# A Fourier operator's 3x3 convolution: 64-column matmuls on a doubled halo, and 32x32 taps on a halo that holds each pixel once

## What is computed

```python
h = concatenate([grid, x], -1) @ P_w + P_b                  # 5 -> 32 channels
h = transpose(h, (0, 3, 1, 2))
for i in range(4):
    h_ft = rfft2(h)                                         # only 16x16 modes are used
    out_modes = einsum('bixy,ioxy->boxy', h_ft[:, :, :16, :16], w_c[i])
    spec = irfft2(out_modes, s=(64, 64))
    conv = conv_general_dilated(h, conv_w[i], (1, 1), 'SAME') + conv_b[i]    # 3x3, 32 -> 32
    h = leaky(spec + conv)
h = leaky(transpose(h, (0, 2, 3, 1)) @ Q1_w + Q1_b)
out = (h @ Q2_w + Q2_b)[..., 0]
```

## Time and profile before

| | us |
|---|---|
| median of 3 runs | 1379.96 (1377.09 to 1383.61) |
| the profiled execution | 1379.42 |
| its span | 1377.6 |
| TensorE busy | 1248.0 (91%) |
| VectorE (DVE) busy | 541.0 (39%) |
| ScalarE (ACT) busy | 493.1 (36%) |
| GpSimd (POOL) busy | 66.8 (5%) |

### The profile page before, as it was taken

How to read it: one execution, slowest core, us unless ns; L and a number is a source line. 1 busy time by engine, 2 the same in 40 slices (tenths; PEclk the granted TensorE clock), 3 DMA queues, 4 the chain that set the end, 5 groups by cost and what they waited for, 6 DMA issues and landing times. The chain is left out here.

```text
span 1377.6 us, 42277 instructions
## 1 busy us (share of the span) xinstructions
PE 1248.0 (91%) x19664; PEld 709.5 (52%) x19664; DVE 541.0 (39%) x553; ACT 493.1 (36%) x934; POOL 66.8 (5%) x122
## 2 busy tenths in 40 slices
PE   4899997999999998999999989999999943799955
PEld 2566664555555555545555554434444413489945
DVE  3656753333353334333353322110111104667785
ACT  1255654033333332233333333334444432425511
POOL 2000000000000000000000000011111110000000
PEclk9999998999999999999999999999999976979967
DMA  8354547667666776766666663556655407000000
GB/s 279 140 158 132 147 159 190 217 192 190 191 190 191 191 190 219 191 190 191 190 192 193 191 187 74 121 130 129 129 121 116 89 3 157 0 1 1 1 0 16
DMA packets 39359, 192.53 MB, mean 140 GB/s; under 512 B 16432, under 2 KB 16560, under 8 KB 17456
## 3 DMA queue, kind: packets, MB, share of 16 engines
q1 hardware_dynamic: 30224, 137.39, 40.3%
q0 software_dynamic: 8960, 52.44, 10.5%
HBM read 136.84 MB, written 52.95 MB: 138 GB/s over the span
## 5 line engine op out<-in xcount | busy, mean ns | idle before, releaser
L376 PE MATMUL psum<-halo,conv 128*64 128x512 f32 x2304 | 516.2, 598 | 2.8 <-DMA halo<-activations 2.6
L504 ACT ACTIVATE x_now<-psum,conv_bias 128x512 f32<-128x512 f32 x256 | 172.9, 688 | 525.4 <-PE psum L387 508.1
L376 PEld LDWEIGHTS psum<-halo,conv 128*64 128x64 f32 x2304 | 157.5, 136 | 322.0 <-issue 318.6
L574 DVE STREAM_TRANSPOSE ft<-psum 128x1024 f32<-128x1024 f32 x50 | 98.3, 1966 | 380.3 <-PE psum L290 380.3
L387 PE MATMUL psum<-dft,vt 128*32 128x128 f32 x8192 | 241.0, 273 | 0.7 <-issue 0.6
L387 PEld LDWEIGHTS psum<-dft,vt 128*32 128x32 f32 x8192 | 220.7, 110 | 39.0 <-issue 39.0
L597 DVE STREAM_TRANSPOSE vt<-psum 128x1024 f32<-128x1024 f32 x64 | 126.0, 1969 | 249.3 <-PE psum L352 249.3
L487 ACT ACTIVATE spec<-psum 32x128 f32<-32x128 f32 x384 | 147.2, 383 | 40.3 <-PE psum L303 36.4
L567 DVE STREAM_TRANSPOSE xt<-x_now 128x1024 f32<-128x1024 f32 x100 | 124.0, 1242 | 34.0 <-ACT x_now L504 28.2
L352 PE MATMUL psum<-zt,dft 64*32 64x256 f32 x2048 | 78.2, 380 | 5.4 <-DVE zt L590 5.4
L511 ACT ACTIVATE xt<-psum,q1b 128x512 f32<-128x512 f32 x64 | 40.5, 683 | 106.8 <-PE psum L401 106.8
(11 more groups left out here) (133 smaller groups left out, 776.5 us busy)
## 6 DMA issues: line engine op xcount, KB each, us to landing
activations<-x_now POOLq DMA_DIRECT2D x48, 1056.0 KB, 8.7
halo<-activations SPq DMA_DIRECT2D x192, 264.0 KB, 7.4
halo<-activations SPq DMA_DIRECT2D x192, 263.9 KB, 7.6
wspec<-in_spec SPq DMA_DIRECT2D x16, 1024.0 KB, 9.6
xcol<-in_xcol SPq DMA_DIRECT2D x16, 384.0 KB, 4.5
x_now<-in_ser SPq DMA_DIRECT2D x2, 1056.0 KB, 6.7
t_lq<-in_onehot SPq DMA_DIRECT2D x1, 2048.0 KB, 14.8
t_kr<-in_causal SPq DMA_DIRECT2D x1, 2048.0 KB, 24.9
```

Of the source, the lines that this page charges most:

```text
L376: mm(acc[u][64 * r:64 * r + 64, :], conv[:, l - 1, dy, :], rows[:, at:at + 16, 0:G], start=(dy == 0), stop=False, skip_group_check=True)
L504: copy(x_now[:, k, 16 * u:16 * u + 16, 0:G], acc[u].rearrange("p (i j) -> p i j", j=G), ACT.Prelu, bias=conv_bias[:, l:l + 1], alpha=SLOPE ...
L574: vec.transpose(ft[:].rearrange("p k c -> p c k"), rowed.rearrange("p a b -> p (a b)").rearrange("p (i c) -> p c i", c=C)).then_inc(s_ft, 1)
```

## The change

Three things change together. First, the convolution's form: each of the 9 taps is a matmul of 32 input channels by 32 output channels for each of the four pixel parities and each of the four banks, 144 matmuls a tile at the 16 positions of the array. Input parity f goes to output parity f ^ d, where d tells whether the tap changes the row parity (2) and the column parity (1); the taps of one d form a segment, with 4, 2, 2 and 1 taps for d = 3, 1, 2 and 0. So that the four parities of a bank fall on different array rows and columns, bank u keeps its parities in the order parity ^ u ("turn"), and spectral, rows_forward, the head and the loads follow that. The halo holds each pixel once, with the same partitions as x_now.

Second, the order on TensorE: the four segments stand between the other groups of the tile. Since a segment d > 0 writes the places that the one before wrote from other array rows, it waits for it (s_seg). taps(T, 3) writes all four banks and waits for all four evictions of tile T - 1. The banks 0 and 1 are reported as finished (s_acc) by taps(T, 0) together.

Third, the transfers: a tile is stored with 4 DMAs of 264 KB, one per bank, the last two not before the next tile's segment 3 is done. It is loaded with 16 DMAs of 66 KB, 8 after segment 1 of the tile before and 8 after its segment 2. The next layer's weights go out 1 MB at a time in the tiles p = 2, 4, 6 and 8, and negate, which needs them, stands at p = 12 and not at p = 8. head_read is one activation of 128 partitions, and it stands before all of the tile's evictions.

The diff, cut to its core:

```diff
-PAD = 2 * PITCH
-HALO = 2 * PLANE + PAD
+UNIT = 16 * PITCH
+TOP = 1 + 2 * PITCH
+HALO = TOP + PLANE + 2 * PITCH + 1
...
-            def load_halo(T):
+            def load_halo(T, units):
                 l, p = place(T)
-                k, src = T % 2, T - PAIRS
-                sp.wait_ge(s_store[src % 2], 16 * (src // 2 + 1))
...
-                                     ).then_inc(s_halo[k], 16)
+                k = T % 2
+                for u in units:
+                    for f in range(4):
+                        g = 32 * (f ^ turn(l - 1, u))
+                        sp.dma_start(halo[32 * f:32 * f + 32, k, TOP + UNIT * u:TOP + UNIT * u + UNIT],
+                                     x_d[p, g:g + 32, UNIT * u:UNIT * u + UNIT]).then_inc(s_halo[k], 16)
...
-            sp.wait_ge(s_zero, 3)
-
...
-                    load_halo((l + 1) * PAIRS)
+            sp.wait_ge(s_zero, 2)
+
+            sp.wait_ge(s_mix, 4)
+            for p in range(2, PAIRS):
+                sp.wait_ge(s_acc, 4 * (p - 2) + 4)
+                load_columns(p)
+                if p % 2 == 0 and p // 2 <= 4:
+                    load_weights(1, p // 2 - 1)
+            for T in range(PAIRS, NL * PAIRS):
+                l, p = place(T)
+                src = T - PAIRS
+                sp.wait_ge(s_store[src % 2], 64 * (src // 2 + 1))
+                if T < PAIRS + 2:
+                    load_halo(T, range(4))
+                else:
+                    sp.wait_ge(s_seg, 3 * (T - 1 - PAIRS) + 2)
+                    load_halo(T, (0, 1))
+                    sp.wait_ge(s_seg, 3 * (T - 1 - PAIRS) + 3)
+                    load_halo(T, (2, 3))
+                if l < NL - 1 and p in (2, 4, 6, 8):
+                    if p == 2:
+                        sp.wait_ge(s_mix, 4 * l + 4)
+                    load_weights(l + 1, p // 2 - 1)
...
             def store(X):
-                pool.wait_ge(s_x, 4 * X + 4)
-                pool.dma_start(x_d[X % PAIRS], x_now[:, X % 2].rearrange("p i j -> p (i j)")
-                               ).then_inc(s_store[X % 2], 16)
+                for u in range(4):
+                    pool.wait_ge(s_x, 4 * X + u + 1)
+                    if u == 2 and X >= PAIRS - 1:
+                        pool.wait_ge(s_seg, 3 * (X + 1 - PAIRS) + 1)
+                    pool.dma_start(x_d[X % PAIRS, :, UNIT * u:UNIT * u + UNIT],
+                                   x_now[:, X % 2, 16 * u:16 * u + 16].rearrange("p i j -> p (i j)")
+                                   ).then_inc(s_store[X % 2], 16)
...
-                for m in range(2):
-                    for h in range(2):
...
-                                   xt[64 * r:64 * r + 64, 32 * h + m:32 * h + 32:2, :], start=True, stop=True)
+                l = (n - 2) // PAIRS if n >= 2 else 0
+                for i in range(2):
+                    for m in range(2):
+                        for h in range(2):
+                            for f in range(2):
+                                u, g = 2 * h + i, 64 * m + 32 * h
+                                at = 16 * u + m
+                                z = mm(rowed[g:g + 32, f ^ (turn(l, u) // 2), 256 * i:256 * i + 256],
+                                       ex[64 * f:64 * f + 64, turn(l, u) % 2, :],
+                                       xt[64 * f:64 * f + 64, at:at + 15:2, :], start=True, stop=True)
...
-            def convolve(T, u):
+            def convolve_first(T):
+
+                k, p = T % 2, T % PAIRS
+                pe.wait_ge(s_xcol[k], 16 * (p // 2 + 2))
+                for u in range(4):
+                    reached(pe, s_x, 4 * (T - 1) + u + 1)
+                    mm(acc[u], conv0[:], xcol[:, k, HALF * u:HALF * u + HALF], start=True, stop=False,
+                       skip_group_check=True)
+
+            def taps(T, d):
 
                 l, p = place(T)
                 k = T % 2
-                reached(pe, s_x, 4 * (T - 1) + u + 1)
-                if l == 0:
...
-                           start=(dy == 0), stop=False, skip_group_check=True)
+                if d == 3:
+                    pe.wait_ge(s_x, 4 * T)
+                    pe.wait_ge(s_halo[k], halo_loads(T))
+                else:
+                    pe.wait_ge(s_seg, 3 * (T - PAIRS) + {1: 1, 2: 2, 0: 3}[d])
+                for dy in ((-1, 1) if d & 2 else (0,)):
+                    for dx in ((-1, 1) if d & 1 else (0,)):
+                        w = 3 * (dy + 1) + dx + 1
+                        for u in range(4):
+                            for f in range(4):
+                                to, r, s = f ^ d ^ u, (f ^ d) // 2, (f ^ d) % 2
+                                di, dj = (r + dy - f // 2) // 2, (s + dx - f % 2) // 2
+                                at = TOP + (16 * u + 2 * di) * PITCH + dj
+                                rows = halo[32 * f:32 * f + 32, k, at:at + UNIT].rearrange("p (i j) -> p i j", j=PITCH)
+                                z = mm(acc[u][32 * to:32 * to + 32, :], conv[32 * f:32 * f + 32, l - 1, w, :],
+                                       rows[:, :, 0:G], start=(d == 3 and dy == -1 and dx == -1), stop=False,
+                                       skip_group_check=True)
+                if d > 0:
+                    z.then_inc(s_seg, 1)
+                elif p > 0:
+                    z.then_inc(s_acc, 2)
 
             def spectral(T, u):
 
+                l, p = place(T)
                 k = T % 2
                 pe.wait_ge(s_vt, T + 1)
                 for ih in range(4):
                     for r in range(2):
                         for s in range(2):
-                            g = 64 * r + 32 * s
+                            g = 32 * ((2 * r + s) ^ turn(l, u))
                             z = mm(acc[u][g:g + 32, 128 * ih:128 * ih + 128], vt[:, k, 4 * u + ih, r, :],
                                    ix[:, s, :], start=False, stop=True, skip_group_check=True)
-                z.then_inc(s_acc, 1)
+                if u >= 2 or l == 0 or p == 0:
+                    z.then_inc(s_acc, 1)
...
-            def pair(l, p, last):
+            def first_pair(p):
+
+                T = p
+                if p > 0:
+                    convolve_first(T)
+                    rows_forward(T + 1)
+                    if p < LAST:
+                        columns_back(T + 1)
+                for u in range(4):
+                    spectral(T, u)
+                if p > 0:
+                    columns_forward(T + 1)
+                else:
+                    columns_back(T + 1)
+
+            def pair(l, p):
 
                 T = l * PAIRS + p
-                if p > 0:
+                if p == 0:
                     for u in range(4):
-                        convolve(T, u)
-                        if last and u % 2 == 0:
-                            head_hidden(p - 1, u)
-                    if not last:
-                        rows_forward(T + 1)
+                        spectral(T, u)
+                    columns_back(T + 1)
+                    return
+                taps(T, 3)
+                rows_forward(T + 1)
                 if p < LAST:
                     columns_back(T + 1)
-                for u in range(4):
-                    spectral(T, u)
...
-                    columns_forward(T + 1)
+                taps(T, 1)
+                spectral(T, 0)
+                taps(T, 2)
+                spectral(T, 1)
+                taps(T, 0)
+                spectral(T, 2)
+                spectral(T, 3)
+                columns_forward(T + 1)
+
+            def last_pair(p):
+
+                T = (NL - 1) * PAIRS + p
+                if p == 0:
+                    for u in range(4):
+                        spectral(T, u)
+                    columns_back(T + 1)
+                    return
+                taps(T, 3)
+                head_hidden(p - 1, 0)
+                taps(T, 1)
+                head_hidden(p - 1, 2)
+                taps(T, 2)
+                head_out(p - 1)
+                spectral(T, 0)
+                spectral(T, 1)
+                taps(T, 0)
+                spectral(T, 2)
+                spectral(T, 3)
+                if p < LAST:
+                    columns_back(T + 1)
+
+            def boundary(l):
+
+                T = l * PAIRS
+                taps(T, 3)
+                rows_forward(T + 1)
+                taps(T, 1)
+                columns_forward(T + 1)
+                pe.wait_ge(s_spec, T + 2)
+                mix(l)
+                columns_back(T)
+                taps(T, 2)
+                taps(T, 0)
...
-                for u in range(4):
-                    z = copy(h_now[32 * u:32 * u + 4, k, :], valued[32 * u:32 * u + 4, :], ACT.Identity,
-                             bias=q2b[32 * u:32 * u + 4, :])
-                z.then_inc(s_h, 1)
+                copy(h_now[:, k, :], valued, ACT.Identity, bias=q2b[:]).then_inc(s_h, 1)
...
                     for u in range(4):
                         head_activate(p - 1, u)
```

(8 more changed lines are left out.)

125 lines of the change are left out of this document (39 added, 86 removed).

## The result

The changed kernel took 1549.38 us (median of 4 runs, 1543.5 to 1553.9) against 1380.16 for the kernel before on the same chip: ratio 1.1223, 95% interval 1.1173 to 1.1272. The prediction was 1346 in a range of 1300 to 1386. The profiled execution took 1553.9 us, with a span of 1552.1, 174.5 more than before. Two executions further down, one of wide loads and one of taps innermost, ran slower than the others of their kernel at a lower granted clock; the medians and ratios leave them out.

A forecast was written before the change was run, and what follows sets the result against it. TensorE, busy 91% of the span, was taken to bound the kernel. 1379.42 - 48.3 (layers 1 and 2) - 6.1 (layer boundaries) - 28.2 (last layer) - 2.0 (end) + 51 (late halo loads) = 1345.8; forecast 1346 us, range 1300 to 1386.

The forecast's parts named there:

- The sixteen positions run side by side: Convolution taps: 18 steps of 0.429 us, 7.72 us; the rival that they do not had chance 0.08.
- the rule about one PSUM bank: Taps: different row tiles cannot access one bank simultaneously; a step would be 1.71 us, the total some 2400; one in a hundred.
- The prediction's own sign of being wrong: Ahead of taps(3) in layers 1 and 2: an idle gap over 2.8 us, where 1.2 to 2.2 was expected.
- The halo loads come too late: Before taps(3), layers 1 and 2 and first tiles of layers 2 and 3: 1.7 us a tile, 30 times, +51 us.
- the upper bound: Halo stall before taps(3): 3.5 us a tile, landing in 3.3 with one more us of backpressure, 105 us.
- Loads slower still: Rival at the halo loads: from a stall of 2.8 us nothing is gained, at 3.5 it is 1400; chance 0.10.
- Changes of shape: Switching between tap segments in the convolution: 0.22 us allowed for each of four segments, 0.88 us a tile.
- The gain of 48 us: Layers 1 and 2: tile without waits from 17.10 to 15.49 us, 1.61 less in 30 tiles, -48.3 us.
- 28 predicted: Last layer, 15 tiles: -1.88 us a tile after a wait on evictions, -28.2 us.
- predicted at none by 0.4 us: Last layer's halo loads: 9.8 us of work against a start at 9.35, so hidden.
- the tower's end: At the very end, one head eviction in place of four at 0.68 lies on the path: -2 us.
- the sum: Whole kernel: 1379.42 us before, with all predicted terms applied, gives 1345.8 us.

The follow-up runs named there:

- wide loads: Changed kernel, gates kept, units side by side in memory loaded in one DMA (4 issues a tile in layer 1, 11 in layers 2 and 3): 1396.8 us, ratio 1.009.
- taps innermost: Changed kernel with loads waiting only until tile T-2 has left the buffer, plus taps looped inside units and row groups: 2774.6 us, ratio 2.01.
- late stores: Changed kernel, load gates kept, no unit of a tile stored before taps(3) of the next tile has ended: 1514.0 us, ratio 1.091.
- Filler: Changed kernel with five unread 128x512 matmuls added ahead of taps(3) in layers 1 and 2, tiles p = 2 to 15: 1511.0 us, ratio 1.089.
- Free loads: Changed kernel with halo loads waiting only until tile T-2 has left the buffer, not for segments 1 and 2 of tile T-1: 1367.5 us, ratio 0.986.

## Why the prediction was wrong

**Right.** The sixteen positions run side by side (a step is 0.43 us), so the rule about one PSUM bank that the prediction quotes from the Trainium skill (TensorEngine Tiling (Array Packing), Restrictions and Gotchas), given one in a hundred, does not show here. The loads do come too late, in layers 1 and 2 and in nearly every tile, and by the mechanism named: sixteen issues against the work that is left. That work was predicted at 7.9 us and is 8.24 (316.64 to 324.88). The prediction's own sign of being wrong, a gap over 2.8 us, stood in 27 of the 28 tiles p = 2 to 15.

**The step that failed** is the one under "The halo loads come too late", in three ways, all to the slow side.

- *Its size.* In the tile shown, from the end of taps(1): last issue predicted at 7.15, measured 10.2 (326.8); start of taps(3) predicted 9.35, measured 12.75. I took 0.465 us for each issue, from the median, though the row beside it had a maximum of 2.04 us, and put in one microsecond of backpressure only at the upper bound. In the mean of the 28 tiles sixteen issues took 9.29 us where 7.4 was predicted (the median is 0.42 us, the mean 0.53; before the change the halo's issues already had a mean of 0.65), and the last load landed 3.14 us after its issue, not 2.35: 2.1 is what the median load takes. The stall is 3.8 us in their mean, over my bound of 3.5. Wide loads shows that the number of issues decides, late stores that the stores take about a tenth, through the landings.
- *What stands behind it.* I priced a wait as idle time. The kernel before ran these layers at a granted clock of 1.00 with next to no wait; behind a stall of some 4 us the work is mostly slower. Over 30 tiles (the 28 and two at layer boundaries) that is 50 us, and 3 more in the last layer, in two tiles behind gaps of 2.52 and 3.07 us. Filler shows it: 46 us of slow taps gone in its 28 tiles, for 128 us of useless work. Layers 1 and 2 close with it: 115.1 us of halo waits + 49.9 of slow taps are 165.0, measured 158.4; the other 6.6 were gained, about 4 by the shorter tiles and 3 by the piece behind the first mixing product.
- *The rivals.* "Loads slower still" was named, with its break-even at 2.8 us, and given 0.10 with a price of 1400 at 3.5. Its arithmetic gives 1409 at the measured 3.8. Without the clock that price was too low by 50.

**Mis-sized** was the gain. "Changes of shape" allowed 0.22 us a segment, and the steps 18 x 0.429 with nothing between two taps. Each further tap of a segment costs more: 10.04 us for the convolution, not 8.60, so 17.06 (the usual tile before) became 16.93 and not 15.49. The gain of 48 us was 4 to 5. The hidden product, from which I took the switch, has one tap's worth of passes and could not show what a second costs. In the last layer the clean tile is 17.25 against 18.33, 16 us for 28 predicted, and the halo's waits there (22.3 us), predicted at none by 0.4 us, took more than that. That the last layer still ends even is owed to the tower's end, which became some 8 us shorter, for 2 predicted, and to the piece behind the last mixing product.

By these terms: 86 us of halo wait over the 51, 53 of clock, 43 of taps in layers 1 and 2 and 12 in the last layer, and 15 behind the tower, 209 in all, against 208 between the sum and the profiled execution. That it closes so well is in part luck: the tower's end came out some 6 us better than forecast, the boundaries and layer 0 some 4 worse, and neither is in these terms.

**Free loads says what the change is worth**: its profiled tower ends at 1122.3 where that of before ended at 1140.0, 18 us sooner, of the 84 of array work and evictions predicted. The taps' further rounds took 43 and 12 of the difference and the pauses some 13. So the gate turned a small gain into a large loss, and the array's gain was over-forecast besides.

**Open.** Why about two of sixteen issues take 1.0 to 2.4 us, while the median stays at 0.42 (late stores excludes the stores beside them), why instruction blocks come late now and then, why the clock fell behind some gaps and not behind others of the same length, and the 14.6 us of the token stages. No run here settles these.

## What to carry to other kernels

Before a load is tied to an event late in the iteration before it, count issues times the *mean* issue time (with its outliers), add the slowest landing, and set it against the work left; when that is within a few microseconds, gate earlier (here: no gate for half of the loads and taps(3) for the rest). In this kernel, whose granted clock was 1.00, stalls of 3.8 us in the mean cost their idle time and some 40% again behind it (50 us on 115), those of 1.5 us in the mean some 14% (3 on 22). Packed 32x32 matmuls run side by side only as far as the queue reaches: put the loop over positions innermost, and price each further round from a row that has two.

## What the runs showed of the hardware that was not expected

- The order of the same matmuls is worth a factor of 6.8 on a segment (29.78 against 4.40 us): by the starts a position takes at most four passes, and the queue about 32.
- TensorE itself seems to wait for its next 256 instructions at times, 0.6 to 3.7 us where I counted, at full clock, once with the DMA engines at 3% and once with them full. It is most frequent in the variants whose loads are wide or freed, with 67 thousand instructions in all (33 in four runs), and absent from their last layer; the kernel before, with 42 thousand, has four. The Trainium skill (Runtime: NRT & Kernel Launch, Instruction fetch mechanics) has the refill in blocks of 256 and calls its cost mostly hidden; the 3.5 us of 572.53 to 576.03 was not.
- A DMA issue on SP has a median of 0.42 us whether it moves 66 or 264 KB, and single ones of up to 2.36.
